# Parts of q and k stored and loaded one by one, and VectorE's maxima moved ahead of its other work in four slots

## The reference, cut to what matters

```python
q = proj(layernorm(x), Wq, bq); k = proj(ctx, Wk, bk); v = proj(ctx, Wv, bv)   # 16 heads of 16
q = q * cos + rotate_half(q) * sin          # k likewise
scores = einsum('bhqd,bhkd->bhqk', q, k) / 4
scores = where(|query - key| <= 50, scores, -1e9)
out = softmax(scores) @ v
x = x + tanh(g_xattn) * (out @ Wo.T + bo)
x = x + tanh(g_ffn) * ffn(layernorm(x))     # 16-bit activations, 4-bit weights, quantized
```

## Time and profile before

| | us |
|---|---|
| Median of 3 runs | 1368.07 (1368.03 to 1373.25) |
| The profiled execution | 1368.83 |
| its span, first to last instruction | 1367.1 |
| PE busy | 1203.8 |
| VectorE busy | 1212.9 |
| ScalarE busy | 826.5 |
| GpSimd busy | 549.5 |
| Mean granted clock of TensorE | 0.965 of full |

### The profile page before, as it was taken

One profiled execution on the slowest core, in us unless ns is written; L12 is line 12 of the kernel. 1 busy time (PEld: TensorE's weight loads), 2 busy tenths in 40 slices (PEclk: granted clock), 3 DMA queues, 4 the chain that ended last, 5 costly groups with the idle time before them and its releaser, 6 DMA issues. The chain is left out here.

```text
span 1367.1 us, 27802 instructions
## 1 busy us (share of the span) xinstructions
PE 1203.8 (88%) x8963; PEld 786.5 (58%) x8995; DVE 1212.9 (89%) x3603; ACT 826.5 (60%) x1336; POOL 549.5 (40%) x1357
## 2 busy tenths in 40 slices
PE   5689898989998988998988659998999799968998
PEld 3457666666666666666666434443433334427887
DVE  3799999999999999999998849997999989988886
ACT  2255656666666665656565536665677599983332
POOL 1177777777777777777776610000000000000000
PEclk9699999999999999999999869999999999988999
DMA  2757575757565666666664202223455455546764
GB/s 78 156 121 183 135 174 139 168 139 164 143 161 146 158 151 153 154 151 158 146 161 112 102 8 93 111 97 127 158 183 185 159 191 196 199 165 205 241 225 169
DMA packets 132369, 207.27 MB, mean 152 GB/s; under 512 B 11159, under 2 KB 97050, under 8 KB 126106
## 3 DMA queue, kind: packets, MB, share of 16 engines
q1 hardware_dynamic: 132250, 205.86, 54.4%
HBM read 125.60 MB, written 79.69 MB: 150 GB/s over the span
## 5 line engine op out<-in xcount | busy, mean ns | idle before, releaser
L670 DVE CUSTOM_DVE_ANT_0 psum<-psum,band 128x178 f32<-128x178 f32 x1024 | 316.5, 372 | 38.4 <-PE psum L878 38.1
L552 ACT ACTIVATE probs<-psum 128x356 f32<-128x356 f32 x512 | 210.6, 468 | 162.7 <-PE psum L895 162.2
L486 POOL TENSOR_SCALAR_AFFINE_SELECT probs<-probs 128x154 f32<-128x154 f32 (+1 forms) x512 | 221.4, 443 | 156.5 <-ACT probs L552 150.5
L1088 PE MATMUL psum<-xnT,w_upT 128*128 (+1 forms) x1152 | 261.1, 384 | 19.0 <-DVE maxima L1312 8.8
L1088 PEld LDWEIGHTS psum<-xnT,w_upT 128*128 128x128 f16 x1152 | 109.9, 99 | 170.0 <-issue 32.6
L878 PE MATMUL psum<-k_stack,q_stack 96*128 96x178 bf16 x1024 | 141.3, 245 | 51.3 <-DVE smax L670 47.4
L495 POOL TENSOR_SCALAR_AFFINE_SELECT probs<-probs 128x254 f32<-128x254 f32 (+1 forms) x512 | 180.3, 375 | 0.0
L895 PE MATMUL psum<-q_stack,k_stack 98*128 98x178 bf16 x1024 | 136.2, 242 | 16.8 <-DMA q_stack<-shiftT 10.5
L670 DVE DVE_READ_ACCUMULATOR2_ANT smax<- 128x1 f32 x1024 | 142.9, 140 | 0.0
L1688 PE MATMUL psum<-w_downT,xnT 128*128 128x256 f16 x1152 | 128.3, 275 | 16.0 <-DVE xnT L1638 16.0
L878 PEld LDWEIGHTS psum<-k_stack,q_stack 96*128 96x128 bf16 x1024 | 74.2, 98 | 109.0 <-DVE smax L670 87.2
(11 more groups left out here) (189 smaller groups left out, 2265.3 us busy)
## 6 DMA issues: line engine op xcount, KB each, us to landing
k_parts_scratch<-k_parts SPq DMA_DIRECT2D x32, 384.0 KB, 2.5
q_parts_scratch<-q_parts SPq DMA_DIRECT2D x32, 384.0 KB, 2.6
k_stack<-k_parts_scratch SPq DMA_DIRECT2D x32, 384.0 KB, 5.1
q_stack<-q_parts_scratch SPq DMA_DIRECT2D x32, 384.0 KB, 7.3
gate_scratch<-g_stage SPq DMA_DIRECT2D x16, 768.0 KB, 3.2
g_in<-gate_scratch SPq DMA_DIRECT2D x16, 768.0 KB, 4.6
sig_scratch<-w_gateT SPq DMA_DIRECT2D x32, 384.0 KB, 2.3
sig_again<-sig_scratch SPq DMA_DIRECT2D x32, 384.0 KB, 3.4
```

The costliest lines, as they stand in the source:

```text
L486: nc.gpsimd.affine_select(out=t[:, :, 0:n], in_=t[:, :, 0:n], pattern=[[0, 2], [1, n]], compare_op=ALU.is_ge, fill=0.0, base=WINDOW - off, ...
L552: nc.scalar.activation(ring_tile(probs, b, pair, c)[:].rearrange("p e j -> p (e j)"), scoreT_bank[c][:, 0:2 * SPAN], ACT.Exp, scale=DK ** ...
L670: ins = nc.vector.tensor_tensor_reduce(out=mine, in0=mine, in1=keep["band"][:, t, :], scale=1.0, scalar=-3e38, op0=ALU.add, op1=ALU.max, a ...
L1088: last = nc.tensor.matmul(bank[:], weights[wp][:, c * I + f * P:c * I + (f + 1) * P], x_parts[:, c, bass.ds(j * (2 * TILE) + xp * TILE, TI ...
```

## The change

1. Stores: `store_parts` becomes `store_part`, one transfer of 128 KB for each part, each waiting for its own part alone. Parts 1 and 2 count on one semaphore (`rest_stored`), part 0 on another (`high_stored`).
2. Loads: `load_stacks` becomes `load_part`. q's part g goes with one transfer (48, 32, 16 partitions, as before). k's stack is filled by part: part 0 in three transfers of 16 partitions, part 1 in two, part 2 in one. Part 0 waits for its own store, parts 1 and 2 for the stores of both.
3. SP's order is rewritten: 15 issues for q and k in place of 8.
4. VectorE: in slots 3 to 7 the maxima come ahead of rotation of q (slot 3), remainder of k (4), low part of k (5), low part of q (6) and statistics (7). The remainder of q (5) and the shift parts stay ahead.
5. GpSimd makes the scale in slot 0 of the batch's own step rather than in slot 7 of the one before.
6. ScalarE: V is copied in slot 4, ahead of the exponentials; the middle parts of k and q come behind the exponentials of slots 4 and 5.

```diff
-            def store_parts(b, n):
+            def store_part(b, n, part):
                 if not b.real:
                     return
-                reached(sp, mid_ready[n], b, 1, 1)
-                reached(sp, low_ready[n], b, 1, 1)
+                reached(sp, part_ready[n][part], b, 1, 1)
                 if b.n >= NBUF:
-                    sp.wait_ge(stack_loaded[n][b.buf], b.rnd * 48)
-                sp.dma_start(scratch[n][b.buf].rearrange("k (a d) (h t) -> (d h) (k a) t", a=2, h=H),
-                             parts[n][:].rearrange("p k (a t) -> p (k a) t", a=2)).then_inc(parts_stored[n], 16)
+                    sp.wait_ge(stack_loaded[n][b.buf], b.rnd * LOADED[n])
+                sp.dma_start(scratch[n][b.buf, part].rearrange("(a d) (h t) -> (d h) a t", a=2, h=H),
+                             parts[n][:, part, :].rearrange("p (a t) -> p a t", a=2)).then_inc((rest_stored if part else high_stored)[n], 16)
...
+                if part:
+                    reached(sp, rest_stored[n], b, 32, 32)
+                else:
+                    reached(sp, high_stored[n], b, 16, 16)
+                    reached(sp, scoredT, b.before(NBUF), 2 * PAIRS, 2 * PAIRS)
                 row = 0
                 for g in range(3):
                     rows = (3 - g) * DK
+                    if n == "q" and g == part:
+                        sp.dma_start(stack[row:row + rows, :, :].rearrange("r s t -> r (s t)"),
+                                     scratch[n][b.buf, part].unsqueeze(1).to_broadcast([DK, 3 - g, H * S]))\
+                            .then_inc(stack_loaded[n][b.buf], 16)
+                    if n == "k" and part < 3 - g:
+                        sp.dma_start(stack[row + part:row + rows:3 - g, :, :].rearrange("r s t -> r (s t)"),
+                                     scratch[n][b.buf, part]).then_inc(stack_loaded[n][b.buf], 16)
                     row += rows
...
                 load_residual(Batch(rnd, unit, 3))
+                store_part(Batch(rnd, unit, 0), "k", 0)
                 load_shift(Batch(rnd, unit, 2), 1)
-                store_parts(Batch(rnd, unit, 0), "k")
-                store_parts(Batch(rnd, unit, 0), "q")
-                load_stacks(Batch(rnd, unit, 0), "k")
-                load_stacks(Batch(rnd, unit, 0), "q")
+                b0 = Batch(rnd, unit, 0)
+                store_part(b0, "k", 1)
+                load_part(b0, "k", 0)
+                store_part(b0, "k", 2)
+                store_part(b0, "q", 0)
+                load_part(b0, "k", 1)
+                load_part(b0, "k", 2)
+                load_part(b0, "q", 0)
+                store_part(b0, "q", 1)
+                store_part(b0, "q", 2)
+                load_part(b0, "q", 1)
+                load_part(b0, "q", 2)
                 load_shift(Batch(rnd, unit, 1), 0)
...
-                    if slot == 7:
-                        scale_of(Batch(rnd, unit, -1), moments_taken, scale_steps, scale_ready, moments, scale_small, scale)
+                    if slot == 0:
+                        scale_of(Batch(rnd, unit, 0), moments_taken, scale_steps, scale_ready, moments, scale_small, scale)
...
                         copy_outT(b3, 1)
-                        middle(b0, "k")
                         high(b0, "q")
-                    if slot == 5:
...
                             copy_out(b0, projected["v"], 1, 1, bank_b[:].rearrange("p (h d) -> p h d", d=DK),
                                      v_heads(b0.buf)[:, :, 0:DK], v_copied, [(weighted, b0.before(NBUF), PAIRS, PAIRS)])
-                        middle(b0, "q")
...
+                    if slot == 4:
+                        middle(b0, "k")
+                    if slot == 5:
+                        middle(b0, "q")
...
                     if slot == 3:
                         shift_parts(b2, 1)
+                    if slot == 5:
+                        remainder(b0, "q")
+                    if slot == 7:
+                        shift_parts(b1, 0)
+                    pair, late = pair_at(slot, S_FIRST)
+                    maxima(Batch(rnd, unit, late), pair)
+                    if slot == 3:
                         rope(b0, "q", bank_a)
                     if slot == 4:
                         remainder(b0, "k")
                     if slot == 5:
                         low(b0, "k")
-                        remainder(b0, "q")
                     if slot == 6:
                         low(b0, "q")
-                    if slot == 7:
-                        shift_parts(b1, 0)
-                        if nxt.real:
-                            reached(dve, x_loaded, nxt, 16, 16)
-                            statistics(nxt, x_in, stats, moments, stats_taken, moments_taken)
-                    pair, late = pair_at(slot, S_FIRST)
-                    maxima(Batch(rnd, unit, late), pair)
+                    if slot == 7 and nxt.real:
+                        reached(dve, x_loaded, nxt, 16, 16)
+                        statistics(nxt, x_in, stats, moments, stats_taken, moments_taken)
```

More of the change, by code:

```diff
@@ L277, in attention @@
         xres_loaded = [sem(f"xres_loaded{k}") for k in range(NBUF)]
-        parts_stored = {n: sem(f"{n}_parts_stored") for n in "qk"}
+        high_stored, rest_stored = ({n: sem(f"{n}_{size}_stored") for n in "qk"} for size in ("high", "rest"))
         stack_loaded = {n: [sem(f"{n}_stack_loaded{k}") for k in range(NBUF)] for n in "qk"}
@@ L298, in attention @@
         mid_ready = {n: sem(f"{n}_mid_ready") for n in "qk"}
+        part_ready = {n: (high_ready[n], mid_ready[n], low_ready[n]) for n in "qk"}
         shiftT_copied, exp_done = sem("shiftT_copied"), sem("exp_done")
@@ L317, in attention @@
         rows_c = ctx_in.rearrange("b (t p) d -> b p t d", p=P)
+        LOADED = {"q": 16 * 3, "k": 16 * 6}
         def run(steps):
@@ L390, in load_residual, with load_part @@
                 sp.dma_start(x2[b.buf][:], rows_x[b.n]).then_inc(xres_loaded[b.buf], 16)
-            def store_parts(b, n):
+            def store_part(b, n, part):
                 if not b.real:
                     return
-                reached(sp, mid_ready[n], b, 1, 1)
-                reached(sp, low_ready[n], b, 1, 1)
+                reached(sp, part_ready[n][part], b, 1, 1)
                 if b.n >= NBUF:
-                    sp.wait_ge(stack_loaded[n][b.buf], b.rnd * 48)
-                sp.dma_start(scratch[n][b.buf].rearrange("k (a d) (h t) -> (d h) (k a) t", a=2, h=H),
-                             parts[n][:].rearrange("p k (a t) -> p (k a) t", a=2)).then_inc(parts_stored[n], 16)
-            def load_stacks(b, n):
+                    sp.wait_ge(stack_loaded[n][b.buf], b.rnd * LOADED[n])
+                sp.dma_start(scratch[n][b.buf, part].rearrange("(a d) (h t) -> (d h) a t", a=2, h=H),
+                             parts[n][:, part, :].rearrange("p (a t) -> p a t", a=2)).then_inc((rest_stored if part else high_stored)[n], 16)
+            def load_part(b, n, part):
                 if not b.real:
@@ L407, in load_stacks @@
                 stack = (q_stack if n == "q" else k_stack)[b.buf]
-                reached(sp, parts_stored[n], b, 16, 16)
-                reached(sp, scoredT, b.before(NBUF), 2 * PAIRS, 2 * PAIRS)
+                if part:
[3 more added lines that the diff above has]
+                    reached(sp, scoredT, b.before(NBUF), 2 * PAIRS, 2 * PAIRS)
                 row = 0
@@ L412, in load_stacks @@
                     rows = (3 - g) * DK
-                    sp.dma_start(stack[row:row + rows, :, :].rearrange("r s t -> r (s t)"), scratch[n + "_rows"](b.buf, g)).then_inc(stack_loaded[n][b.buf], 16)
+                    if n == "q" and g == part:
[5 more added lines that the diff above has]
+                                     scratch[n][b.buf, part]).then_inc(stack_loaded[n][b.buf], 16)
                     row += rows
@@ L534, in high @@
                 reached(act, rotated[n], b, 1, 1)
-                reached(act, parts_stored[n], b.before(1), 16, 16)
+                reached(act, high_stored[n], b.before(1), 16, 16)
+                reached(act, rest_stored[n], b.before(1), 32, 32)
                 nc.scalar.activation(parts[n][:, 0, :], rot[n][:], ACT.Copy).then_inc(high_ready[n], 1)
@@ L700, in round_weight @@
                 if m == 0:
-                    dve.wait_ge(parts_stored["q"], 16 * B)
+                    dve.wait_ge(high_stored["q"], 16 * B)
+                    dve.wait_ge(rest_stored["q"], 32 * B)
                 if n == "w_down":
@@ L870, in scores @@
                 if pair == 0:
-                    pe.wait_ge(stack_loaded["k"][b.buf], b.rnd * 48 + 48)
-                    pe.wait_ge(stack_loaded["q"][b.buf], b.rnd * 48 + 48)
+                    pe.wait_ge(stack_loaded["k"][b.buf], (b.rnd + 1) * LOADED["k"])
+                    pe.wait_ge(stack_loaded["q"][b.buf], (b.rnd + 1) * LOADED["q"])
                 for t in range(T):
@@ L1707, in build @@
     for n in "qk":
[L1709 to L1718, removed]
```

(1 more changed line is left out.)

## The result

The changed kernel takes 1476.26 us (median of 3, 1475.85 to 1482.03), 1.0785 times the kernel before, interval 1.0746 to 1.0825: 108 us slower. The forecast was 1407 with a range from 1358 to 1432. The direction was right, and so was the loop that it named; the sizes of that loop's terms were too small.

The account below looks back on a forecast made before the run. VectorE's order of work was taken to set the 22.48 us period; after the change, transfers would, at 7.25+16.6=23.85 us. Taking 1.2 us a step, 31x1.2=37 plus 1 on 1368.8 gave 1407 us, range 1358 to 1432.

Parts of the forecast that it names:

- transfer loop: Attention loop from scoresT through SP's stores and loads to the next scoresT: 23.85 us a step; chance 0.60 for 23.0 to 24.6.
- part (3): Prediction's pricing of SP's queue, fifteen issues one by one: 7.25+16.6=23.85 us a step, longer than the old 22.48.
- chain of transfers: SP's queue, from issuing the store of k's part 1 to the shift rows: 16.6 us; 14.4 with least prices, 18.8 with greatest.
- start-ups: Time before a load's first group of 16 stack rows lands: taken as 2.1 us, between 1.9 and 2.9; each group then 0.76.
- stretch from scoresT to k's part 1: From PE's scoresT at 315.90 to SP's issue of the store of k's part 1 at 323.15: 7.25 us.
- 1.2 us a step, a little under 1.37: Loss per attention step: taken as 1.2 us instead of 23.85-22.48=1.37, because least prices pull down for some loads.
- greatest prices: Upper bounds for transfers in SP's queue, with start-up 2.9 us: 18.8 us from k's part 1 to the shift rows.
- heavy chain: Rival in SP's queue: start-up 2.9 us each time, 18.8 us, a loop of 26, 1480 us; above 1432 has chance 0.10.
- the 1 us allowed for the first batch: First batch: k's middle part comes behind q's high part and V, costing up to 3 us, taken as 1.
- Stores do not overtake loads: SP's queue: stores wait for loads queued ahead; the opposite case, last loads at about 14 us and 1358 us, had chance 0.06.
- compute loop of 22.1 us: Engines' own attention loop in the new order: 22.1 us, 0.36 less than 22.48, as PE no longer waits at scores(7).
- the 3.1 us for the scale and for normalising: From 308.94 to PE's transpose of xn at 312.05: 3.1 us, counted as enough for GpSimd's four operations and normalising.

## Why the prediction was right or wrong

- **Where the time goes: right.** The forecast put 0.60 on a transfer loop of 23.0 to 24.6 us behind scoresT of pair 0, with two landings in series; time line and waits show it link by link, and exchanging the links takes it away.
- **Its size: wrong**, and outside the range. By its own part (3) the period was 23.85; it is 25.73. Two terms of the sum failed, the landings in the chain and the stretch ahead of it.
- **The chain of transfers, 16.6 us: it took 17.83**, within the bounds of 14.4 and 18.8. Of the missing 1.24 us, 0.82 are landings of loads: 5.03 us from k's part 1 to its first three groups (forecast 4.85), 7.14 from the issue of the six remaining groups (6.65), 4.55 for q's last three (4.4). If a group keeps its 0.76, the start-ups come out at 2.3, 2.6 and 2.3 us where the forecast took 2.1; that is an estimate. The fixed cost of about 2 us that the forecast names from the Trainium skill ("DMA: Bandwidth & Descriptors", Anatomy of one DMA) is fitted there to transfers that GpSimd issues; SP issues these. Another 0.3 are stores behind loads: k's part 2 landed 0.22 us behind the load ahead (0.1), q's second store 0.57 (0.4). The shift rows cost 0.29 behind the last load (0.1).
- **The stretch from scoresT to k's part 1, 7.25 us: it took 7.90.** The other 0.65 is the slow clock, in a term that I gave no range at all. It was read from a trace in which the attention part ran at a granted clock of 0.99. The forecast itself said that PE would wait 1 to 2 us a step and did not ask what a waiting PE does to its own speed.
- **"1.2 us a step, a little under 1.37"** cut the sum without a row for it; that was 5 us. The range ended at a loop of 24.5, though the forecast's own greatest prices made 26 and 1480 us. This heavy chain had 0.10 with all else above 1432; its 1480 is near the measured 1476 in part by luck, since the chain took 17.8 and not 18.8; the clock and the drain, which it did not have, made up for that.
- **The steps.** Between the rotation of k of the first and of the last batch, 31 steps, the kernel lost 98 us (27.94 to 818.06, against 27.66 to 719.45), 3.2 a step; the first four lost 11 together, no more than the others. The steps that drain the pipeline lost another 9, for which the forecast had nothing. Added up over 31 steps, chain 38, clock 20, the cut 5 and the drain 9 make 72, against the 69 us that the forecast was short; the 1 us allowed for the first batch was not needed.
- **Stores do not overtake loads: right, closely.** k's part 2 always landed behind the loads ahead of it. The first of q's last two stores landed some 0.2 us ahead of the last of those loads in 20 of 24 steps, the second always behind it.
- **The compute loop of 22.1 us: not reached.** With the transfers mostly out of the way (stores first, or stores on ScalarE's queue) no step was under 22.3 us, and the means were 22.7 and 22.5, against 22.5 for stores first with the old order of work, which was 8 us faster. The reading that the change gives up what it wins, since q's rotation moved onto the path to ScalarE's packed stretch, fits GpSimd's wait for VectorE's product of q (22.0 us in the waits above, 0.4 before), but no run takes that one move back alone. Nor were the 3.1 us for the scale and for normalising enough: PE's transpose of xn waits 0.5 us a step for ScalarE (7.2 us in 15 steps), which it did not before.
- **The order of work as a cause: missed.** I worked out that k's part 1 would be later, and used it, but not that this order alone, with whole transfers, costs 50 us.
- The smaller marks: k's remainder fell to 0.78 us on average (1.47 before, 200 to 600 us); PE's wait for the copy of V is gone; VectorE's largest wait stands ahead of slot 3's maxima, as forecast (2.68 us in the step shown), and 1.04 us are left in slot 0.

## What to carry to other kernels

In an in-order queue of transfers, draw the chain of landings before the bytes: a store whose landing a load waits for should not stand behind other loads; exchanging lines of the queue gave back 102 of 108 us here with every transfer unchanged. Issuing two stores from another engine, which reached them 5.5 us sooner, gave the same; they landed no faster for it. When two halves of a change lie in one loop, their costs aren't additive: price the loop, not the halves. And give every term of the loop a range, those of the engines too: a wait that you forecast for PE may slow what PE does next.

## What was not expected of the hardware

- With waits of about 2.7 us in each step TensorE's granted clock over the attention part was 0.94 (200 to 760 us), 0.99 before, and 0.55 in the 3.3 us behind the wait shown. After another wait of the same 2.43 us it stayed at 1.00.
- A store of 128 KB landed 1.8 us after its issue (median of k's stores where they stand first), 2.7 and 2.9 us from ScalarE's and from SP's queue behind the same three groups of loads, 4.2 in the changed kernel (median of q's three, two of which stand behind six groups).
